# Cross-attention of a decoder layer on Trainium2: another order of head quads, one stretch of score matmuls, input transposes and gelu moved within the step

## What is computed

```
x = x + self_attention(layernorm(x))                 # 16 heads of 8, rotary, causal
x = x + cross_attention(layernorm(x), ctx, ctx)      # 16 heads of 8, ctx: 64 x 77 x 128
x = x + moe_ffn(layernorm(x))                        # 8 experts by low-rank deltas, top 2
```

```
qk = Q K^T;  scores = qk / sqrt(8);  probs = softmax(scores)
feats  = [mean(scores), mean over queries of max(scores), mean over queries of var(probs)]   # per head
hidden = gelu(feats w1^T + b1);  hidden = gelu(hidden w2^T + b2)
t      = exp(clip(hidden w3^T + b3))                 # one temperature per sequence and head
out    = softmax(qk / (2 t)) V;  return out Wo^T + bo
```

## Time and profile before

| | us |
|---|---|
| median of 3 runs | 1714.31 |
| the profiled execution, own time | 1719.28 |
| its span, first to last instruction | 1717.5 |
| of it, from step 9 to the end of step 61 | 503.89 |
| PE busy over the span | 1642.8 (96%) |

### The profile page before, as it was taken

The page is one execution under the profiler, slowest core; times in us unless marked ns, Lnnn a source line. Parts: engine busy times, 40 slices in busy tenths (PEclk is TensorE's granted clock), DMA queues, the critical chain, the costliest instruction groups (busy, mean ns, idle before and its releaser), DMA issues. The chain is left out here.

```text
span 1717.5 us, 42620 instructions
## 1 busy us (share of the span) xinstructions
PE 1642.8 (96%) x14336; PEld 1223.2 (71%) x14336; DVE 1235.7 (72%) x2888; ACT 926.2 (54%) x2189; POOL 880.2 (51%) x1006
## 2 busy tenths in 40 slices
PE   6999999999978999999999999897999999999998
PEld 2555555555546666666666666557999999999998
DVE  5887777777646767766677776436878878787886
ACT  3555545555433666666566666545454545545452
POOL 3444455544446767776677777412433434343342
PEclk9999999999958999998999999788999999999999
DMA  4000000000000000000000000100000000000000
GB/s 123 13 3 2 1 1 1 1 1 1 6 5 4 7 7 7 6 7 6 6 7 7 7 7 5 43 2 1 11 6 9 6 9 6 9 9 6 9 6 13
DMA packets 27869, 16.62 MB, mean 10 GB/s; under 512 B 6193, under 2 KB 25586, under 8 KB 27762
## 3 DMA queue, kind: packets, MB, share of 16 engines
q1 hardware_dynamic: 27762, 15.23, 3.2%
HBM read 9.97 MB, written 4.19 MB: 8 GB/s over the span
## 5 line engine op out<-in xcount | busy, mean ns | idle before, releaser
L1555 POOL TENSOR_TENSOR ff_zz<-ff_zt 128x256 f32<-128x256 f32 x32 | 37.5, 1173 | 318.2 <-DVE ff_zt L1759 318.2
L278 POOL TENSOR_TENSOR sa_KM<-sa_HQK,sc_headmask 128x512 fp32r<-128x512 f32 x64 | 66.7, 1042 | 235.6 <-ACT sa_HQK L318 235.6
L964 ACT ACTIVATE xa_P<-xa_SK 77x1024 f32<-77x1024 f32 x128 | 130.2, 1017 | 98.1 <-PE xa_SK L1287 97.9
L1623 ACT ACTIVATE ff_SG<-bank 128x512 f32<-128x512 f32 x128 | 76.6, 599 | 189.3 <-PE bank L1836 189.3
L1749 DVE TENSOR_TENSOR ff_GL<-ff_GU,ff_GH 128x512 fp32r<-128x512 f32 x128 | 148.6, 1180 | 27.2 <-ACT ff_GH L1628 27.2
L323 ACT ACTIVATE sa_P<-sa_SK 128x1024 f32<-128x1024 f32 x128 | 131.5, 1028 | 59.1 <-PE sa_SK L515 59.1
L409 DVE TENSOR_REDUCE sa_mx<-sa_SQ 128x8 f32<-128x1024 f32 x128 | 156.7, 1224 | 7.6 <-PE sa_SQ L515 5.3
L890 POOL TENSOR_TENSOR xa_QMH<-xa_QBH,xc_headmask 128x512 fp32r<-128x512 f32 x64 | 72.6, 1135 | 151.2 <-ACT xa_QBH L954 151.2
L1901 PE MATMUL bank<-fh_r,ff_GH 128*128 128x256 f32 x512 | 149.2, 292 | 0.0
L1834 PE MATMUL bank<-ff_ZH,fh_b 128*128 128x256 f32 x512 | 146.2, 286 | 0.0
L1903 PE MATMUL bank<-fh_r,ff_GL 128*128 128x256 f32 x512 | 144.5, 282 | 0.0
(11 more groups left out here) (259 smaller groups left out, 5398.3 us busy)
## 6 DMA issues: line engine op xcount, KB each, us to landing
xa_shift<-xa_row SPq DMA_DIRECT2D x256, 2.0 KB
out<-X SPq DMA_DIRECT2D x64, 64.0 KB, 1.5
cx<-ctx SPq DMA_DIRECT2D x64, 38.5 KB
sa_shift<-sa_mT SPq DMA_DIRECT2D x64, 8.0 KB, 1.8
X<-x SPq DMA_DIRECT2D x1, 768.0 KB, 6.7
xa_E<-L_ffn_B SPq DMA_DIRECT2D x2, 256.0 KB, 3.7
xa_E<-down_a SPq DMA_DIRECT2D x1, 512.0 KB, 4.4
X<-x SPq DMA_DIRECT2D x1, 256.0 KB, 2.9
```

Of the source, the lines that this page charges most:

```text
L964: nc.scalar.activation(P[0:TC, (2 * b + h) % 4, :], SK[0:TC, :], ACT.Exp).then_inc(p_ready, 1)
```

## The change

1. The four quads of a sequence are held in the order (2, 1, 3, 0) in tile SQ and all that is made from it; `rows` and the constant `headsel` follow. Places 0-3 and 8-11 of the score tile are now row groups 2 and 3, places 4-7 row group 1, places 12-15 row group 0.
2. `scores_outer` makes places 0-3 and 8-11 alone; `scores_inner` makes 12-15 as well, its first part ahead of the wait for `outer_ps`; it follows directly on `scores_outer`.
3. `xc_transpose(n+2)` is issued within `by_key(n-7, 0)`, after the two matmuls that add the shift.
4. `mlp1` comes ahead of `pv(n-8, 1)`, and `max_transpose(n)` ahead of all of `by_key(n-7, 1)`; `mlp3` stays behind its first two matmuls.
5. On ACT, `scaled` and `xcT_copy` come ahead of `exps(n-7, 0)`.

The waits of each function stay as they were. The diff, cut:

```diff
+CROSS_ORDER = (2, 1, 3, 0)
...
-                for g in range(QUADS):
+                for place, g in enumerate(ORDER):
                     sp.dma_start(shift[32 * g:32 * g + 1, b % 2].bitcast(F32),
-                                 row[JH * g:JH * g + JH].bitcast(F32)).then_inc(m_row[b % 2], 16)
+                                 row[JH * place:JH * place + JH].bitcast(F32)).then_inc(m_row[b % 2], 16)
...
                 r = mlp_round(n)
-                if real(n - LAG):
-                    exps(n - LAG, 0)
                 if real(n - LAG + 1):
                     scaled(n - LAG + 1)
                 if real(n + 2):
                     xcT_copy(n + 2)
+                if real(n - LAG):
+                    exps(n - LAG, 0)
                 if r is not None:
                     gelu1(r)
...
-                g = first_head // JH
+                g = ORDER[first // JH]
...
                 for part in range(3):
-                    scores(b, 0, 4, part, part == 0, part == 2)
-                    scores(b, 8, 12, part, part == 0, part == 2)
-                    last = scores(b, 12, 16, part, part == 0, part == 2)
+                    scores(b, 0, 4, part)
+                    last = scores(b, 8, 12, part)
                 last.then_inc(outer_ps, 1)
 
             def scores_inner(b):
+                scores(b, 12, 16, 0)
                 pe.wait_ge(outer_ps, b + 1)
                 for part in range(3):
-                    scores(b, 4, 6, part, False, part == 2)
-                    last = scores(b, 6, 8, part, False, part == 2)
+                    if part > 0:
+                        scores(b, 12, 16, part)
+                    scores(b, 4, 6, part)
+                    last = scores(b, 6, 8, part)
                 last.then_inc(sq_ps, 1)
...
                 for a, _, r in quads:
                     mm(bank(SK, a), pick[:, r // 32], shift[:, b % 2].rearrange("c j t -> c (j t)"),
                        start=True, stop=False)
+                if early is not None:
+                    xc_transpose(early)
...
-                    if part == 0 and between is not None:
-                        between()
+                    if part == 0 and third is not None:
+                        mlp3(third)
...
+                early = n + 2 if real(n + 2) else None
                 if real(n - LAG):
-                    by_key(n - LAG, 0)
+                    by_key(n - LAG, 0, early)
+                elif early is not None:
+                    xc_transpose(early)
                 if real(n):
                     scores_outer(n)
+                    scores_inner(n)
+                if r is not None:
+                    mlp1(r, n)
                 if real(n - LAG - 1):
                     pv(n - LAG - 1, 1)
-                if r is not None:
-                    mlp1(r, n)
-                if real(n + 2):
-                    xc_transpose(n + 2)
-                if real(n):
-                    scores_inner(n)
                 if real(n + 2):
                     qkv(n + 2)
...
+                if 2 <= n < LAG:
+                    filler(SK[:, 512:1024], 6)
+                if real(n):
+                    max_transpose(n)
                 if real(n - LAG):
-                    by_key(n - LAG, 1, maxima)
-                else:
-                    if 2 <= n < LAG:
-                        filler(SK[:, 512:1024], 6)
-                    maxima()
+                    by_key(n - LAG, 1, None, r)
+                elif r is not None:
+                    mlp3(r)
```

More of the change, by code:

```diff
@@ L631, in cross_attention @@
     HIDDEN = slice(3 * T, 3 * T + GROUP * H)
+    ORDER = CROSS_ORDER
     ctx = ExitStack()
@@ L1226, in _, with scores @@
             PARTS = ((HQ, KMH), (HQ, KML), (LQ, KMH))
-            def scores(b, first_head, last_head, part, start, stop):
-                g = first_head // JH
+            def scores(b, first, last, part):
+                g = ORDER[first // JH]
                 rows = slice(32 * g, 32 * g + 32)
                 queries, keys = PARTS[part]
-                at = first_head // 6 * 512 + first_head % 6 * TC
-                j = first_head % JH
-                n = last_head - first_head
+                at = first // 6 * 512 + first % 6 * TC
+                j = first % JH
+                n = last - first
                 return mm(SQ[:, at:at + n * TC], queries[rows, b % QRING],
-                          keys[rows, b % 2, j:j + n].rearrange("c j k -> c (j k)"), start=start, stop=stop,
-                          skip_group_check=True)
+                          keys[rows, b % 2, j:j + n].rearrange("c j k -> c (j k)"), start=(part == 0 and n == JH),
+                          stop=(part == 2), skip_group_check=True)
             def scores_outer(b):
@@ L1270, in subtract_max, with mlp1, mlp2, mlp3 @@
                 last.then_inc(neg_ps, 1)
-            def by_key(b, h, between=None):
+            def mlp1(r, n):
+                pe.wait_ge(var_ready, GROUP * (r + 1) // 2)
+                pe.wait_ge(sim_ready, r + 1)
+                pe.wait_ge(max_ready, 2 * GROUP * (r + 1))
+                need(pe, onT_sb, n - LAG - 1)
+                if r == 0:
+                    pe.wait_ge(prepared, PREPARED + 1)
+                for f in range(3):
+                    last = mm(R[0:64, HIDDEN], w1s[:, f, :], of_group(FEAT[:, f], r), start=(f == 0), stop=(f == 2))
+                last.then_inc(mlp_ps, 1)
+            def mlp2(r):
+                pe.wait_ge(mlp_act, 3 * r + 1)
+                mm(R[:, HIDDEN], w2p[:], h1[:], start=True, stop=True).then_inc(mlp_ps, 1)
+            def mlp3(r):
+                pe.wait_ge(mlp_act, 3 * r + 2)
+                mm(R[:, HIDDEN], w3r[:], h2[:], start=True, stop=True).then_inc(mlp_ps, 1)
+            def by_key(b, h, early=None, third=None):
                 need(pe, p_ready, 2 * b + h)
@@ L1334, in project @@
                 mm(M[:, 0:C], onT[:], wo[:], start=False, stop=True).then_inc(proj_ps, 1)
[L1336 to L1353, removed]
             pe.wait_ge(ones_set, 2)
@@ L2032 @@
     cos, sin = per_head(np.cos(angle)), per_head(np.sin(angle)) * sign
+    heads_in_order = (JH * np.array(CROSS_ORDER)[:, None] + np.arange(JH)[None]).reshape(-1)
     first_row = eye.copy()
@@ L2040 @@
         tri=np.ascontiguousarray(np.broadcast_to(np.tril(np.ones((8, 8), np.float32), -1), (128, 8, 8))),
-        headsel=(np.arange(128)[:, None] // DK == np.arange(H)[None]).astype(np.float32),
+        headsel=(np.arange(128)[:, None] // DK == heads_in_order[None]).astype(np.float32),
         headmask=(np.arange(128)[:, None] // DK % JH == np.arange(JH)[None]).astype(np.float32),
```

## The result

The changed kernel takes 1676.92 us, the median of 4 runs (1673.85 to 1681.42); the kernel before takes 1714.4 beside it (4 runs, 1714.21 to 1716.89). The ratio is 0.9769, with a 95% interval from 0.9747 to 0.9791: faster by 2.3%. Forecast were 1675.0, in a range from 1656 to 1700.

A forecast was written before the change was run, and what follows sets the result against it. PE's order was taken to bound ordinary steps, ACT in a chain with PE the MLP steps. Savings 22.4 + 14.8 - 5.2 + 2 + 5 gave 39 us: 1714.3 - 39 = 1675 us, range 1656 to 1700.

The forecast's parts named there:

- Ordinary step: Step without MLP work, bound by PE's order: from 8.59 to 8.21 us, 0.38 saved despite three new waits.
- The passes: PE, second pass with outer and inner scores until the product with V: 1.95 us, before 2.13.
- The shifts with the wait for the residual: PE ahead of the early transposes: shifts 0.43 us, before 0.64, plus a new wait of 0.2 for the residual add.
- The maxima's wait: PE ahead of the maxima's transpose: a new wait for DVE's reductions of 0.35 us (0.1 to 0.5).
- The second half in one go: PE, second half of the second pass: six matmuls without the maxima's transpose in their midst, 0.76 us.
- MLP step: Step with MLP work, held by ACT in a chain with PE: from 11.46 to 9.85 us, 1.6 saved in each of 14.
- The split in halves: MLP step's saving: half from the earlier gelu table load, half from the maxima's transpose no longer standing behind the shifts.
- The step behind it: Step after an MLP step: DVE's residual add comes later, so PE waits 0.4 us more at the early transposes, 13 times.
- The clock: Of 8.5 us lost at the low clock, 5 gained, since falls lie in MLP steps and the step behind them.
- The steps from 62 on: Steps 7, 8, 62 and 63 save 0.38 us each, the MLP step behind them some 0.6: 2 together.
- rival 2: Row groups do not run side by side, matmuls being strict FIFO: 0.64 us more per step, 1710 us; chance 0.03.
- the residual at "about 1.1": DVE's residual add done no sooner than about 1.1 us into the step: projection 0.50, its result 0.3, add 0.27.

The follow-up runs named there:

- e5: Changed kernel with the output projection in PSUM tile O instead of M, so the early transposes need not wait for the residual add: 1656.2 us.
- e3: Changed kernel with the maxima's transpose put back inside the second half of the second pass: 1696.9 us.
- e2: Changed kernel with the quads in their old order 0, 1, 2, 3: 1711.8 us.
- e9: Changed kernel with `scaled` alone moved back behind `exps` on ACT, `xcT_copy` still ahead of it: 1744.7 us.
- e1: Changed kernel with ACT's old order, `exps` ahead of both `scaled` and `xcT_copy`: 1740.7 us.
- e10: Changed kernel with ACT's old order, as in e1, and POOL's square ahead of the query masks: 1722.7 us.
- e11: Changed kernel with the early transposes of the input between the outer and the inner scores: 1662.5 us.
- e6: Changed kernel with the maxima's transpose between the shifts and the second half, in ordinary steps alone: 1665.6 us.
- e4: Kernel before the change with only ACT's new order: 1775.9 us.

## Why the prediction was right, step by step

- **Ordinary step**: 8.21 forecast, 8.12 measured. The passes came to 1.93 (1.95), the last stretch to 1.45 (1.45). The shifts with the wait for the residual were 0.71, forecast as 0.43 + 0.20; without the wait they take 0.55 (e5), so the matmuls were put too low by 0.12 and the wait, 0.16, nearly right. So the first transpose stands 1.21 behind the projection, not 1.1. Of the 0.64 that the shifts took before, 0.09 and not 0.21 goes away when full-array matmuls follow them. The maxima's wait is 0.22 (0.35), the transpose behind it 0.03 (0.17), since the shifts follow it at once. The second half in one go took 0.89 (0.76); with the transpose that is 0.92 against 0.93, two errors that cancel.
- **MLP step**: 9.85 forecast, 9.75 measured. The exponential was to begin 2.5 in (2.52), the load at 3.5 (3.55), gelu1 at 4.8 (4.85), `mlp2` at 5.3 (5.32), the maxima's transpose at 5.65 (5.68), their copy at 6.1 (6.00). The split in halves was not right: e3, with the load where it is after and the maxima's place of before, has 10.83, so the maxima's place is worth 1.08 of the 1.71, and the load and all the rest 0.63.
- **The step behind it**: 0.4 more than an ordinary one was forecast, 0.57 measured, and e5 shows that it is that wait.
- **The clock**: 5 of 8.5 forecast as gained, 4.3 measured, on the premise that the falls lie at MLP steps. In the steps of the sum: 14 x 1.71 = 23.9 (22.4), 39 x 0.48 - 13 x 0.57 = 11.3 (14.8 - 5.2 = 9.6), the clock 4.3 (5): 39.5 against 37.0.
- **The steps from 62 on** gained 4.8, with what lies ahead of step 9 5.3; forecast were 2. The time at 1.2 GHz there went from 24.6 to 13.7 us, which no term of the sum held.
- **The order of execution.** By the rule of rival 2 a step would have been longer by 0.64. The scores again start beside the second pass (774.91 beside 774.89), and e2, which only puts the quads in order, costs 0.34 a step: the order of quads does what it says.
- **Missed**: the change's effect over POOL and DVE. The prediction had the earlier `scaled` only make room ahead of the table load. It is worth 1.1 of each ordinary step under the new PE order (e9): without it the early transposes would have waited as in e1, and steps 9 to 61 would have taken 517 or 522, more than before the change. The forecast held because it counted the residual at "about 1.1" from the projection alone, and took DVE as there in time: in the changed kernel that is so, but only because of this move. To that extent a right forecast was luck: nothing in its working says why DVE is in time. The row of the cast at 0.57 in the median, beside 0.20 at its least, stood in the trace of before and was not read.
- **The noise**: the prediction had a measurement tell 3.4 us, 0.2%, from no change, on three runs within 0.3 us. Beside the experiments the kernel before took from 1709.9 to 1727.4. The 37.5 gained are well above that; a few us between the medians of two experiments are not.

Still open is what brings the clock down. It is not the length of the steps: by the table, four steps at full clock take 34.7 after (three falls), 36.0 in e2 (ten), 36.1 in e3 (none) and 37.2 in e10 (three). Nor is it the idle time of PE alone, since the MLP steps of e3 have 0.9 of it and none fell. The counts are of one execution each: the ten of e2 took from 1707.5 at a mean clock of 0.963 to 1727.9 at 0.948. No run was made to find it.

## What to carry to other kernels

A matmul moved ahead takes its wait with it: ask who releases the wait at the new place, and put between them work that neither uses, as e11 and e6 do, or give the output another bank, as e5 does. Two orders on two engines that meet at semaphores are one change: PE's half of this one costs 25 us alone, ACT's half 60, and both gain 37.5. Before an operation is moved on one engine, look through the queues of the others for what waits for it, and for the operations whose duration varies from one execution to the next within the trace: their least and median say what they collide with.

## What the runs showed of the hardware

- DVE's cast of 128 x 77 float32 takes 0.20 alone and 1.37 when it begins 0.92 into a POOL operation of 2.24 (e1); in the kernel before it mostly began 1.7 into it and took 0.57. Both times it ended 0.05 or 0.06 behind POOL's. The Trainium skill, page "SBUF — State Buffer", section "SBUF: two separate sides", says of the ports that the two engines share that one holds them as an exclusive lock for a whole instruction; the trace agrees for this cast. Not every DVE operation is held: in the changed kernel the maxima's reduction at 776.92 takes 1.12 while the square runs from 777.18, and in e10, where the square is elsewhere, it takes 1.11.
- A table load runs as soon as the ACT engine comes to it, ahead of the wait of the ACTIVATE behind it, and that ACTIVATE then starts 0.02 behind its end (785.05 + 1.28 = 786.33, start 786.35). Here the load began while PE still made that ACTIVATE's input: `mlp1` ran from 784.93 to 785.49.
- Matmuls on free row groups start ahead of others that were issued before them, in each timeline of PE read here; in e11 the outer scores start 0.02 behind the second pass's first pair.
- The clock's share can be as large as the path's: 10 us beside 18 in e2, at least 40 beside at most 20 in e4.
